# Layer 1's attention: projection jobs run as halves in separate steps, casts and norm sums on GpSimd, bias products 128 rows deep

## What is computed

```python
q = einsum('btd,hdk->bhtk', hidden, Wq) + bq      # 16 heads of 16, k and v alike
weights = softmax(q @ k.T / sqrt(16))
out = weights @ v
norms = norm(out, axis=-1)                         # mean over batch and tokens, by head
denom = maximum(norms.mean(axis=(0, 2)), 1e-5)
y = sum_over_heads((out / denom) @ Wo + bo) * gate / H
...
y = h @ w2 + b2;  out = gelu(y @ next_w + next_b)  # experts: 8 of them
```

## Time and profile before

| | us |
|---|---|
| median of 3 runs (2021.01 to 2028.9) | 2028.18 |
| the profiled execution | 2026.51 |
| its span, first to last instruction | 2024.8 |
| PE busy | 1840.7 (91%) |
| DVE busy | 1318.4 (65%) |
| ACT busy | 1178.9 (58%) |
| POOL busy | 580.3 (29%) |

### The profile page before, as it was taken

How to read it: one execution, slowest core, us unless ns; L and a number is a source line. 1 busy time by engine, 2 the same in 40 slices (tenths; PEclk the granted TensorE clock), 3 DMA queues, 4 the chain that set the end, 5 groups by cost and what they waited for, 6 DMA issues and landing times. The chain is left out here.

```text
span 2024.8 us, 29383 instructions
## 1 busy us (share of the span) xinstructions
PE 1840.7 (91%) x10344; PEld 755.3 (37%) x10344; DVE 1318.4 (65%) x2630; ACT 1178.9 (58%) x1621; POOL 580.3 (29%) x720
## 2 busy tenths in 40 slices
PE   4789999999979999999999987899999986699998
PEld 3323333332224444444444442233333222354443
DVE  5478889888743544545535524888888882757673
ACT  4268878876743433333324332788888875567673
POOL 5657777761120000000001012111111100454542
PEclk8589999999989999999999997999999996799998
DMA  3345544444261000000001013333333304323320
GB/s 116 63 91 121 131 119 124 112 108 106 82 233 62 22 22 1 21 16 6 21 7 41 11 36 53 59 74 74 74 74 63 64 12 132 133 96 113 127 63 31
DMA packets 119618, 147.62 MB, mean 73 GB/s; under 512 B 19779, under 2 KB 102838, under 8 KB 117430
## 3 DMA queue, kind: packets, MB, share of 16 engines
q1 hardware_dynamic: 119478, 145.79, 27.3%
HBM read 100.34 MB, written 45.14 MB: 72 GB/s over the span
## 5 line engine op out<-in xcount | busy, mean ns | idle before, releaser
L826 DVE TENSOR_REDUCE A_M<-A_SM 128x1 f16<-128x512 f32 x1024 | 656.0, 683 | 135.7 <-PE A_SM L1043 134.2
L591 ACT ACTIVATE A_P<-A_ST 128x1024 f32<-128x1024 f32 x512 | 524.2, 1026 | 131.3 <-PE A_ST L1059 123.9
L1043 PE MATMUL A_SM<-A_KT,A_QS 48*128 48x512 f16 x1024 | 350.6, 396 | 54.3 <-DVE A_M L826 47.7
L1592 PE MATMUL B_PA<-B_Hh,B_wh 128*128 128x512 f16 x1024 | 388.1, 379 | 0.0
L1592 PE MATMUL B_PA<-B_Hl,B_wh 128*128 128x512 f16 x1024 | 388.1, 379 | 0.0
L1511 ACT ACTIVATE B_af<-B_PA,B_sv 128x512 f32<-128x512 f32 x192 | 132.0, 688 | 354.4 <-PE B_PA L1592 354.2
L1059 PE MATMUL A_ST<-A_QS,A_KT 49*128 49x512 f16 x1024 | 299.1, 387 | 3.0 <-DMA A_QS<-A_rows 2.8
L1076 PE MATMUL A_AV<-A_P,A_V 128*32 128x512 f32 x2048 | 275.9, 611 | 4.4 <-ACT A_P L591 4.1
L1043 PEld LDWEIGHTS A_SM<-A_KT,A_QS 48*128 48x128 f16 x1024 | 85.0, 93 | 438.2 <-DVE A_M L826 380.0
L1555 DVE TENSOR_SCALAR B_Hh<-B_af 128x512 f16<-128x512 f32 x128 | 58.3, 456 | 280.5 <-ACT B_af L1511 280.5
L1306 POOL TENSOR_TENSOR B_hl<-B_hf,B_hh 128x512 f16<-128x512 f32 x14 | 16.2, 1157 | 506.3 <-ACT B_hh L1322 506.3
(11 more groups left out here) (357 smaller groups left out, 3198.5 us busy)
## 6 DMA issues: line engine op xcount, KB each, us to landing
D_w_st<-in_we_dram SPq DMA_DIRECT2D x16, 1024.0 KB, 5.0
qk<-A_tr SPq DMA_DIRECT2D x58, 256.0 KB, 2.5
A_KT<-qk SPq DMA_DIRECT2D x96, 128.0 KB, 4.6
A_QS<-qk SPq DMA_DIRECT2D x96, 128.0 KB, 4.7
A_w_st<-in_w_ffn_dram SPq DMA_DIRECT2D x32, 352.0 KB, 3.3
A_QS<-A_rows SPq DMA_DIRECT2D x512, 0.5 KB
w_hi<-A_f_hi SPq DMA_DIRECT2D x32, 176.0 KB, 3.4
w_lo<-A_f_lo SPq DMA_DIRECT2D x32, 176.0 KB, 3.6
```

The source lines that it names most:

```text
L591: nc.scalar.activation(P[:, st, 2 * pair:2 * pair + 2, :], ST[:, u % 2, :, :], ACT.Exp, scale=1.0 / math.sqrt(HD)).then_inc(exp_s, 1)
L826: nc.vector.tensor_reduce(M[G % 2][:, o:o + 1], SM[:, n % 2, :], AX, ALU.max, negate=True).then_inc(max_s, 1)
L1043: nc.tensor.matmul(SM[:, n % 2, :], QS[b % 2][r, 2 * g + pair, tt * 128:tt * 128 + 128], KT[b % 2][r, 2 * g + pair, :], start=True, stop=T ...
L1592: ins = nc.tensor.matmul(out, a, c, start=start and kt == 0 and n_ == 0, stop=stop and kt == kts[-1] and n_ == len(ops) - 1)
```

## The change

1. The tables `AT1` and `EARLY1` get new steps. Modulo 32: T0 at 1, V0 at 2 and 4, T1 at 9, V1 at 10 and 12, YT1 at 17, QK0 at 18 and 20, QK1 at 23, YT0 at 25, QK2 at 26 and 28, QK3 at 31. A job with two steps runs its part 0 in the first and part 1 in the second (`begun`, `parts`). This holds for batches 2 to 7; batches 0 and 1 keep their steps except for YT.
2. From batch 2 on (`n >= 2`) GpSimd makes the high halves `hh` and `tr` in place of ScalarE.
3. For all groups GpSimd squares the result and sums the 16 squares of a head in four additions (128x128, 128x64, 128x32, 128x16 elements) in place of ScalarE's square and VectorE's reduction.
4. `ones2`, `b2` and `row2` become 128 rows deep, zero below row 2, so that the bias products have 128 rows. Three memsets and two waits are added for it.

```diff
-AT1 = placed(-48, dict(..., T0=-1, T1=1, HH=(0, 2), HL=(1, 3),
-                       QK0=4, QK1=10, QK2=12, QK3=18, V0=20, V1=26, HIGH=(23, 17, ...), LOWS=(25, 20, 26, 20)))
-AT1 |= OUT
+AT1 = placed(-48, dict(..., T0=-15, T1=-7, HH=(-3, -2), HL=(-2, -1),
+                       QK0=(2, 4), QK1=7, QK2=(10, 12), QK3=15, V0=(18, 20), V1=(26, 28),
+                       HIGH=(20, 17, 20, 17, 21, 18, 21, 18), LOWS=(22, 19, 23, 19)))
+AT1 |= dict(YT0=(25,), YT1=(49,))
...
-        b2 = None if L0 else sb("b2", [2, C], F16)
+        b2 = None if L0 else sb("b2", [128, C], F16)
-        ones2 = None if L0 else sb("ones2", [2, 128], F16)
+        ones2 = None if L0 else sb("ones2", [128, 128], F16)
...
+                G = group_at(p, 14)
+                if not L0 and G is not None:
+                    pool.wait_ge(y_out, G + 1)
+                    if G >= 1:
+                        pool.wait_ge(y_norm, G)
+                    nc.gpsimd.tensor_tensor(ysq..., y_, y_, ALU.mult).then_inc(y_sq, 1)
+                    for k, w in enumerate((8, 4, 2)):
+                        pool.wait_ge(...)
+                        nc.gpsimd.tensor_tensor(y_d[:, :, 0:w], y_d[:, :, 0:w], y_d[:, :, w:2 * w], ALU.add).then_inc(y_tree, 1)
+                    nc.gpsimd.tensor_tensor(keep["norm2"][:, G, :], y_d[:, :, 0], y_d[:, :, 1], ALU.add).then_inc(y_norm, 1)
+                for f in range(FT):
+                    n = at(p, "HH", f)
+                    if not L0 and n is not None and n >= 2:
+                        pool.wait_ge(*out(f"T{f}", n))
+                        if f == 0:
+                            pool.wait_ge(*done("V1", n - 1))
+                        nc.gpsimd.tensor_copy(hh_[:, f, :], hf_[:, f, :]).then_inc(h_high, 1)
...
+                        n = at(p, f"QK{i}", late=1)
+                        if n is not None and n >= 2:
+                            pool.wait_ge(*out(f"QK{i}", n))
+                            nc.gpsimd.tensor_copy(tr_[2 * (i // 2)][:, i % 2, :], qkf_[:, i % 2, :]).then_inc(qk_high, 1)
...
-                    for f in range(FT):
+                    for f in parts:                       # QK
-                    for h in range(2):
+                    for h in parts:                       # V
...
-                    job(name, n)
+                    job(name, n, (0, 1) if len(slots_of(name, n)) == 1 else (1,))
+                elif p in begun:
+                    job(*begun[p], (0,))
...
-        rowf, rowh, row2 = sb("rowf", [2, 2, C]), sb("rowh", [2, 2, C], F16), sb("row2", [2, 2, C], F16)
+        rowf, rowh, row2 = sb("rowf", [2, 2, C]), sb("rowh", [2, 2, C], F16), sb("row2", [128, 2, C], F16)
-        ones2 = sb("ones2", [2, 128], F16)
+        ones2 = sb("ones2", [128, 128], F16)
+            nc.gpsimd.memset(row2[:, :, :], 0.0).then_inc(row_zero, 1)
```

More of the change, by code:

```diff
@@ L167, in attention @@
     when = {(name, i, s): n for name in AT for n in range(B) for i, s in enumerate(slots_of(name, n))}
-    when |= {(name, i - len(AT[name]), s): n for (name, i, s), n in when.items()}
+    when |= {(name, i - len(slots_of(name, n)), s): n for (name, i, s), n in when.items()}
     BEGIN, END = slots_of("STAT", 0)[0] - 2 if L0 else -20, PAIRS * B + 30
     names = ["T0", "T1", "QK0", "QK1", "QK2", "QK3", "V0", "V1", "YT0", "YT1"] + (["H0", "H1", "H2", "H3", "P0", "P1"] if L0 else [])
-    jobs = {slots_of(name, n)[0]: (name, n) for name in names for n in range(B)}
-    assert len(jobs) == B * len(names)
+    jobs = {slots_of(name, n)[-1]: (name, n) for name in names for n in range(B)}
+    begun = {slots_of(name, n)[0]: (name, n) for name in names for n in range(B) if len(slots_of(name, n)) == 2}
+    assert len(jobs | begun) == B * len(names) + len(begun)
+    for p in begun:
+        assert not any(q in jobs for q in range(p, slots_of(*begun[p])[1]))
     shared = [job for p, job in sorted(jobs.items()) if job not in own]
@@ L209, in attention @@
         w_ld, w_high, w_split, wp_ld, tab_ld, tab = (sem(n) for n in ("w_ld", "w_high", "w_split", "wp_ld", "tab_ld", "tab"))
-        b_ld, b_high, b_low, b_row, bqk_ld = (sem(n) for n in ("b_ld", "b_high", "b_low", "b_row", "bqk_ld"))
+        b_ld, b_zero, b_high, b_low, b_row, bqk_ld = (sem(n) for n in ("b_ld", "b_zero", "b_high", "b_low", "b_row", "bqk_ld"))
         wm_ld = [sem(f"wm_ld{k}") for k in range(3)]
@@ L549, in step @@
                     for i in range(4):
+                        n = at(p, f"QK{i}", late=1)
+                        if n is not None and n >= 2:
+                            pool.wait_ge(*out(f"QK{i}", n))
+                            pool.wait_ge(kh_st, 16 * n)
+                            pool.wait_ge(qh_st, 16 * n)
+                            nc.gpsimd.tensor_copy(tr_[2 * (i // 2)][:, i % 2, :], qkf_[:, i % 2, :]).then_inc(qk_high, 1)
+                    for i in range(4):
                         n = at(p, f"QK{i}", late=2)
@@ L660, in step @@
                     n = at(p, "HH", f)
-                    if n is not None:
+                    if n is not None and (L0 or n < 2):
                         act.wait_ge(*out(f"T{f}", n))
+                        if not L0 and n >= 1 and f == 0:
+                            act.wait_ge(*done("V1", n - 1))
                         nc.scalar.activation(tile("hh", n)[:, f, :], tile("hf", n)[:, f, :], ACT.Copy).then_inc(h_high, 1)
-                G = group_at(p, 14)
-                if not L0 and G is not None:
-                    act.wait_ge(y_out, G + 1)
-                    if G >= 1:
-                        act.wait_ge(y_norm, G)
-                    g = G % NG
-                    nc.scalar.activation(ysq[:, :].rearrange("p (t c) -> p t c", t=TT), yn[:, :, g * 64:g * 64 + 64],
-                                         ACT.Square).then_inc(y_sq, 1)
                 if not L0:
@@ L674, in step @@
                         n = at(p, f"QK{i}", late=1)
-                        if n is not None:
+                        if n is not None and n < 2:
                             act.wait_ge(*out(f"QK{i}", n))
@@ L869, in step @@
                                             ).then_inc(y_out, 1)
-                G = group_at(p, 16)
-                if not L0 and G is not None:
-                    dve.wait_ge(y_sq, G + 1)
-                    nc.vector.tensor_reduce(keep["norm2"][:, G, :], ysq[:, :].rearrange("p (t d) -> p t d", d=HD), AX, ALU.add
-                                            ).then_inc(y_norm, 1)
                 for tt in range(TT):
@@ L951, in product, with job @@
                 return ins
-            def job(name, n):
+            def job(name, n, parts=(0, 1)):
                 to = bank(name, n)
-                if (name, n) in shared and shared.index((name, n)) >= 1:
+                if 0 not in parts:
+                    pass
+                elif (name, n) in shared and shared.index((name, n)) >= 1:
                     pe.wait_ge(job_out, shared.index((name, n)))
@@ L1026, in job @@
                         (wp_h[:, k, f_], yTh[:, k, :]), (wp_h[:, k, f_], yTl[:, k, :]), (wp_l[:, k, f_], yTh[:, k, :]))], True, True)
-                ins.then_inc(done(name, n)[0], 1)
+                if 1 in parts:
+                    ins.then_inc(done(name, n)[0], 1)
             def raw(n):
@@ L1117, in step @@
                     ins.then_inc(y_mm, 1)
-                if group_at(p, 10) is not None and PAIRS * B - 58 <= p < PAIRS * B - 12 and p not in jobs:
+                if group_at(p, 10) is not None and PAIRS * B - 58 <= p < PAIRS * B - 12 and p not in jobs and p not in begun:
                     free = jobs[max(q for q in jobs if q < p)]
@@ L2067, in _ @@
             dve.wait_ge(row_high, 1)
-            nc.vector.scalar_tensor_tensor(out=row2[:, :, :], in0=rowf[:, :, :], scalar=WS, in1=rowh[:, :, :],
+            dve.wait_ge(row_zero, 1)
+            nc.vector.scalar_tensor_tensor(out=row2[0:2, :, :], in0=rowf[:, :, :], scalar=WS, in1=rowh[:, :, :],
                                            op0=ALU.mult, op1=ALU.subtract).then_inc(row_low, 1)
```

20 lines of the change are left out of this document (13 added, 7 removed).

## The result

| | before | after |
|---|---|---|
| median, us | 2024.60 (6 runs) | 2000.48 (6 runs, 1998.74 to 2011.11) |
| the same in a second comparison, another chip | 2024.28 (11 runs) | 2004.32 (6 runs) |
| ratio, 95% interval | | 0.9892 [0.9858, 0.9925]; second: 0.9895 [0.9875, 0.9914] |
| profiled execution, us (span) | 2026.51 (2024.8) | 2005.26 (2003.6) |
| first `scores` of layer 1 to the last | 422.85 | 411.62 |

The kernel is 1.1% faster: 24.1 us by the first medians, 20.0 by the second, 21.2 by the two profiled executions (15.8 by the second pair of those, before_again and after_again, from which all second traces here come). Forecast were 13.9 less and 2014; 2000.5 lies under the range of 2004 to 2024, the second 2004.3 at its lower end. The sign was right and the size too small.

The account below looks back on a forecast made before the run. Attention was taken as bound by TensorE and VectorE alternating, experts by a chain through TensorE only from gate to the first `project`'s end. Savings 5.1 + 0.9 + 7.0 + 0.9 = 13.9 off 2028.18 gave 2014 us, range 2004 to 2024.

Parts of the forecast that it names:

- Bias products, steady periods: Experts: of eight bias products per period, only the two before z_mm of q = 0 save path time, 0.4 us.
- Six periods: 2.4: Experts: the 0.4 us saved per period by 128-row bias products, taken for six periods, gives 2.4 us.
- The body before them: Experts' body without a `last`, led by TensorE through both `project`s: deeper bias products save 0.8 us.
- The last `last`: End of the experts at a lower TensorE clock: four bias products on the path save 1.0 us.
- First projects and tail: Experts' first `project`s at the lower clock save 0.9 us; attention's end, with YT0 earlier, saves a net 0.9.
- Halves: Layer 1's attention: QK and V jobs split over two steps save 1.17 us a batch, 7.0 over six stretches.
- ScalarE's relief: Attention: squares, casts and a reduction taken off ScalarE and VectorE, counted as 0, with up to 1 possible.
- GpSimd's load: Attention: about 12 us more GpSimd work a batch beside 9.5, of 52, counted as costing 0.
- TensorE bounds the experts: Rival: TensorE bounds the experts throughout, so they save 12.8 us instead of 5.1; 2006.5 us, chance 0.12.
- halves bring nothing: Rival, attention: gain at 4 lost to QK at 7 and a VectorE wait; 7.0 falls away, 2021 us, chance 0.22.
- not absorbed: Rival, attention: halves lengthen their steps with nothing given back; 59.3 us a batch, 2055 us in all, chance 0.10.
- bias products save nothing: Rival: the .2 isn't the change of depth, so only 7.9 us remains; 2020 us, chance 0.05.

Follow-up runs that it names:

- before_again: The kernel before with no edit, traced a second time; its one run took 2019.62 us.
- after_again: The changed kernel with no edit, traced a second time; 15.8 us faster than before_again by the profiled executions.
- bias_only: The kernel before plus only the 128-row bias products; 2010.84 us, ratio 0.9942 to the kernel before.
- both_filled: The kernel before plus dummy products in TensorE's waits ahead of expert 1's second `turn` and the last four bias products; 2017.19 us, ratio 0.9958.
- project_only: The kernel before with 128-row bias products in `project` alone, two rows in attention and `last`; 2015.78 us, ratio 0.9958.
- after_shallow_bias: The changed kernel with bias products two rows deep again; 2015.64 us, ratio 0.9952 to the kernel before.
- norms_only_back: The changed kernel with the norms' squares back on ScalarE and sums on VectorE, casts staying on GpSimd; 2000.57 us, ratio 0.9888 to the kernel before.
- after_whole_jobs: The changed kernel with each halved job run whole in its second step; 2017.77 us, ratio 0.9967 to the kernel before.
- after_filled: The changed kernel plus dummy products in TensorE's waits for `bo` and ahead of the first two `turn`s; 2005.70 us, ratio 0.9902 to the kernel before.
- the filled kernels: The kernel before with dummy products ahead of expert 1's second `turn`, alone (2023.39 us) or also ahead of the last `last` (2017.19 us).

## Why the prediction was wrong

The order of the steps is that of the prediction's sum.

- **Bias products, steady periods: right.** 0.4 of 1.6 on the path; measured 0.41 to 0.43, and the split shows it to be `project`'s, none of it `last`'s.
- **"Six periods: 2.4": the step that failed in the experts.** I took one period of 34.57 for all that have a `last`. The first of these is 37.6 long and led by TensorE, as the second trace of before shows again; a list of all distances of `turn`s in the trace of before had it. All eight bias products lie on the path there (1.57), and 1.40 of clock went with them; forecast 0.4. The four steady periods gave 1.7, the one between 0.66.
- **The body before them, forecast 0.8**: 0.5 and 1.05 in bias_only against the two traces of before (25.94 against 26.45 and 26.99).
- **The last `last`, forecast 1.0: mis-sized.** I costed the change of depth at the low clock that the earlier trace rows show, and didn't ask whether that clock would stay. With 128 rows it is high until TensorE's last product is done (in after it falls at 2002.6, in bias_only at 2002.8, 2.4 us or more behind that product's end): 2.2 and 3.7 saved against the two traces of before. both_filled shows 1.5 and 3.0 of it to be clock.
- **First projects and tail, forecast 0.9 and 0.9: right in sum, the split not shown.** From the last `scores` to the first `turn` 36.86 and 36.0 became 35.43 and 33.8, a mean of 1.8. But bias_only and project_only, with the old tail, take 34.69 and 34.03, and after_shallow_bias, with the new tail and two-row products, 36.31. By these most of the gain is the bias products', and little or none the tail's; that the sum fits is in part luck.
- **Halves, forecast 1.17 a batch and 7.0: right in kind, 1.7 too little.** The four steady stretches of 32 steps gave 1.26 each; but the last two with a V gave 1.81 and 1.89. In the first of these (steps 160 to 191) nothing is left to do for a later batch, neither VectorE's statistics (steps 10, 11, 13 and 14) nor ScalarE's normalisations (22, 24, 26 and 30). The kernel before gains nothing by that (53.65, as in its steady stretches), the changed one does: 1.70 and 1.79 instead of 1.81 and 2.01 in steps 10 and 11, and 5.06 instead of 5.27 in 25 to 27. So in the steady batch this work still stands in the way of the new schedule, and I had multiplied one batch by six. In the last (192 to 223) few jobs of a later batch are left in either kernel, and steps 9 to 11 give 0.70 (5.69 to 4.99), more than in the steady batch. The first 32 steps gave 0.48, of the 0.9 forecast together with the feed-forward part.
- **ScalarE's relief, forecast 0: the verdict was wrong, though the number for the batch was not.** "ScalarE has half a microsecond free in each 1.54 step" averages over steps; behind a whole QK it has none. The whole batch came out at 52.40 against 52.5 since I had computed steps 1 and 25 at 1.57, as if nothing were late: with the casts gone step 1 takes 1.58, and step 25 still 1.79, which the second group's 0.2 made up for. With the casts on ScalarE, halves and bias products together bring 0.49 a batch and not 1.25, less than the 0.61 of the bias products alone. I named the place ("where a job's copy and XN meet") and gave it up to 1, but set 0 for it without following ScalarE's order through it.
- **GpSimd's load, forecast 0: right.** Its queue delays nobody: norms_only_back has the same batch to the hundredth.
- **Clock in the attention and in steady periods: absent from the sum.** The two traces of before lose 2.3 and 1.6 to a stretch at 0.5 inside the attention. Behind the attention's first 13 us, such a stretch is in six of the seven traces with the old steps and two-row bias products there, and in one of the nine others (after_whole_jobs). Against that, the fourth period of the experts takes 35.3 to 35.5 in all four traces that have a batch of 52.4 and 128-row products (after twice, norms_only_back, after_filled), and in none of the other twelve; the second trace of after has it in the fifth too. What the schedule does to bring this about wasn't tried.
- **The base, 3.9 of the miss.** The sum was set on the median of three runs, 2028.18; with 6 to 26 runs the kernel before has 2022.0 to 2025.7. The forecast difference on 2024.3 gives 2010.4.

The account: forecast -13.9. The two pairs of traces, from the first `scores` to the end, average -18.6: attention -11.0 (forecast about -7.5), from there to the first `turn` -1.8 (-1.8), behind it -5.8 (-4.2; -8.5 in bias_only, which has none of the later dips of the clock). Of the -11.0 the six stretches with a V are -8.7, the first one -0.4 and the low clock of before -2.0; without the dips of the changed kernel's own, 1.1 and 3.8 in its two traces, the -5.8 would be -8.2. The medians say -24.1 and -20.0. The 1.4 to 5.5 between are not in any stretch behind the first `scores` of these traces; that part stays open.

Of the rivals, "TensorE bounds the experts" is refuted in the steady periods and true in one; "halves bring nothing", "not absorbed" and "bias products save nothing" are refuted by after_whole_jobs and bias_only. With the casts left on ScalarE the first of these would have come true (53.16 with the halves, 53.04 without). The range's lower end stood on a rival that was wrong, and it had no term for the clock or for periods that are not steady.

## What to carry to other kernels

List every period of a loop before one is multiplied: the first ones may be led by another engine, and an edit that is worth a quarter of its size in the steady state is worth the whole of it there. Where a stretch shows the low clock, cost the edit at both clocks, since which is granted can change with an edit on TensorE's products; a wait that is filled with dummy products is a cheap test of it. Two edits that relieve the same step don't add up, and one that is worth little today (casts off ScalarE: 0.23 a batch) can be what lets another pay (0.76).

## What was unexpected of the hardware

- With the same idle time of 2.80 us ahead of expert 1's second `turn`, the granted clock fell to 0.5 (1.2 GHz) behind it in all five traces in which `project` has two-row products and the wait is unfilled, in neither of the two with the wait filled, and in one of nine with 128-row products (the second trace of after: 35.95). So the rows' depth of the products around an idle time goes together with the clock. The Trainium skill ("TensorE: Matmul & The Clock Gate", Part 1) ties the gate to how busy TensorE has been; the filled kernels agree (36.20 against 37.60). Why two-row products go with the low clock is open: it can be their rows, or the 0.2 us that each of them leaves empty, and no run here separates the two. The added products of the filled kernels were 128 rows deep.
- A clock that came up did not last over the next wait here: with 4.7 us of added products at the experts' start it was high twice (6.8 and 3.5 us), and the first gate behind an unfilled wait of 2.46 was at 1.2 GHz all the same (5.07 us for 12 products of 512 columns, with and without them).
- GpSimd's cast of 128x512 takes .61 against ScalarE's .63, so for this form it is no slower; its square of 128x256 takes .61 against ScalarE's .41, and its subtraction of 128x512 1.16.
